# Two orders of instructions in a softmax-attention pipeline: the copy of the transposed probabilities ahead of the reciprocal on DVE, both heads' exponentials ahead of the copy of y on ACT

## The reference

```python
q = einsum('qdh,bcd->bhcq', Q, x) * sq;  k = ...;  v = ...      # x is the layer-normed input
att = einsum('bhcq,bhCq->bhcC', q, k) / d_query                  # 256 x 256 for each head, causal mask
p = softmax(att, axis=-1)
y = einsum('bhcC,bhCv->bhcv', p, v)
z = einsum('dvh,bhcv->bcd', W, y) * (sqrt(d_embed / d_value) / num_heads)
x = x + z;  x = x + 0.5 * spectral(layernorm(x))
```

## Time and profile before

| | |
|---|---|
| median of 3 runs | 1378.2 us (1377.81 to 1380.24) |
| the profiled execution | 1380.31 us, span 1378.6 us |
| mean granted TensorE clock | 0.994 of full speed |
| PE matmuls busy | 1298.8 us, 94% |
| DVE busy | 1017.6 us, 74% |
| ACT busy | 965.7 us, 70% |
| POOL busy | 586.5 us, 43% |

### The profile page before, as it was taken

The page is one execution under the profiler, slowest core; times in us unless marked ns, Lnnn a source line. Parts: engine busy times, 40 slices in busy tenths (PEclk is TensorE's granted clock), DMA queues, the critical chain, the costliest instruction groups (busy, mean ns, idle before and its releaser), DMA issues.

```text
span 1378.6 us, 38689 instructions
## 1 busy us (share of the span) xinstructions
PE 1298.8 (94%) x11323; PEld 1076.3 (78%) x11331; DVE 1017.6 (74%) x4813; ACT 965.7 (70%) x3377; POOL 586.5 (43%) x913
## 2 busy tenths in 40 slices
PE   5799977999999999999999999999999999999996
PEld 4688866878878787878787878787878787878885
DVE  7977789787777777777777777777777777777774
ACT  4744367587777777777777777777777777777774
POOL 5722157344444444444444444444444444444433
PEclk9999999999999999999999999999999999999999
DMA  8000000000000000000000000000000000000000
GB/s 204 0 1 0 1 0 2 0 2 2 2 10 0 9 0 9 0 9 0 9 0 9 0 9 0 9 0 9 0 9 0 9 0 9 0 9 0 9 1 17
DMA packets 14365, 12.33 MB, mean 9 GB/s; under 512 B 709, under 2 KB 12522, under 8 KB 14058
## 3 DMA queue, kind: packets, MB, share of 16 engines
q1 hardware_dynamic: 14240, 11.19, 3.0%
q10 hardware_dynamic: 10, 0.00, 0.0%
HBM read 7.00 MB, written 4.19 MB: 8 GB/s over the span
## 4 chain that ended last, share of the span: by engine, by line
PE 72%; DVE 13%; issue 9%; ACT 3%; DMA 1%; DVEq 1%; POOL 1%; SPq 1%; ACTq 0%; POOLq 0%
PE ps L1050 12%; PE ps L1020 10%; PE ps L1033 10%; PE ps L1059 9%; PE ps L1005 4%; PE ps L1039 4%; PE ps L1007 4%; PE ps L1006 3%; DVE ps L508 2%; DVE pT L523 2%; PE ps L1040 2%; PE ps L1041 2%; ACT qk_hi L730 2%; DVE neg_max L508 2%; PE ps L934 2%
## 5 line engine op out<-in xcount | busy, mean ns | idle before, releaser
L315 POOL TENSOR_TENSOR pr<-pr,rinv 128x256 f32<-128x256 f32 x256 | 157.4, 615 | 631.3 <-DVE rinv L516 631.3
L744 ACT ACTIVATE pr<-ps,neg_max 128x128 f32<-128x128 f32 (+1 forms) x1024 | 425.0, 425 | 0.0
L508 DVE CUSTOM_DVE_ANT_0 ps<-ps,mask 128x128 f32<-128x128 f32 (+1 forms) x1024 | 334.9, 386 | 0.0
L317 POOL TENSOR_TENSOR pr<-pr,rinv 128x512 f32<-128x512 f32 x256 | 266.9, 1043 | 0.0
L494 DVE TENSOR_TENSOR qk_lo<-ps,qk_hi 128x512 fp32r<-128x512 f32 x256 | 176.5, 689 | 104.2 <-ACT qk_hi L730 103.2
L1050 PE MATMUL ps<-pT,space 128*64 128x256 f32 (+1 forms) x2048 | 223.0, 339 | 24.0 <-DVE pT L523 20.9
L1033 PE MATMUL ps<-ident,pr 128*128 128x128 f32 x1536 | 218.9, 275 | 1.7 <-POOL pr L317 1.6
L744 ACT ACTIVATION_READ_ACCUMULATOR pr<-ps,neg_max 128x1 f32 x1024 | 211.7, 207 | 0.0
L730 ACT CAST qk_hi<-ps 128x512 fp32r<-128x512 f32 x256 | 150.4, 587 | 76.7 <-PE ps L1007 70.7
L1050 PEld LDWEIGHTS ps<-pT,space 128*64 128x64 f32 x2048 | 124.2, 136 | 100.1 <-DVE pT L523 36.3
L1033 PEld LDWEIGHTS ps<-ident,pr 128*128 128x128 f32 x1536 | 174.9, 140 | 34.8 <-issue 11.4
(11 more groups left out here) (165 smaller groups left out, 2398.0 us busy)
## 6 DMA issues: line engine op xcount, KB each, us to landing
out<-x_all SPq DMA_DIRECT2D x16, 256.0 KB, 2.3
x_all<-L_attn_x SPq DMA_DIRECT2D x1, 768.0 KB, 6.2
x_all<-L_attn_x SPq DMA_DIRECT2D x1, 512.0 KB, 3.9
space<-L_attn_Q SPq DMA_DIRECT2D x1, 512.0 KB, 15.3
space<-L_attn_K SPq DMA_DIRECT2D x1, 512.0 KB, 9.5
space<-L_attn_V SPq DMA_DIRECT2D x1, 512.0 KB, 11.3
space<-L_attn_W SPq DMA_DIRECT2D x1, 512.0 KB, 11.7
dft_s<-dft SPq DMA_DIRECT2D x1, 192.0 KB, 2.9
```

Of the source, the lines that this page charges most:

```text
L317: nc.gpsimd.tensor_tensor(pr[:, j, :, 1:3, :].rearrange("p h b k -> p h (b k)"), pr[:, j, :, 1:3, :].rearrange("p h b k -> p h (b k)"), r[ ...
L508: last = nc.vector.tensor_tensor_reduce(o, o, mask[:, T - w:T], -1.0, -MASKED, ALU.add, ALU.min, neg_max[:, j, 2 * h + qt:2 * h + qt + 1])
L744: last = nc.scalar.activation(dst, ps[:, BANK_S + 2 * j + h, qt * P:qt * P + w], ACT.Exp, bias=neg_max[:, j, at:at + 1], scale=-1.0, accum ...
```

## The change

On DVE the copy `probs_T(n-1)` now comes ahead of the reciprocal `inv_sum(n)` in each turn. On ACT both heads' exponentials of pair n+1 now come ahead of the copy of y. No instruction is added or removed, and no wait is changed; each moves with its instruction.

```diff
@@ vector engine, batch()
                     n, j = b * PAIRS + p, p % 2
-                    inv_sum(n, j)
                     if not (first and p == 0):
                         probs_T(n - 1, 1 - j)
+                    inv_sum(n, j)
                     if not (last and p >= PAIRS - 3):
                         qk_low(n + 3, 1 - j)
@@ scalar engine, batch()
                     if not (last and p >= PAIRS - 1):
                         exp_head(n + 1, 1 - j, 0)
+                        exp_head(n + 1, 1 - j, 1)
                     if p > 0:
                         y_out(b, jb, p - 1)
                     elif not first:
                         y_out(b - 1, 1 - jb, PAIRS - 1)
-                    if not (last and p >= PAIRS - 1):
-                        exp_head(n + 1, 1 - j, 1)
```

## The result

The changed kernel takes 1425.1 us (median of 4, 1421.58 to 1427.71), the kernel before 1378.6 in the same session: 1.0334 times as long, 95% interval 1.031 to 1.0359. The profiled execution took 1425.29 us with a span of 1423.5, so it is 45.0 us longer than that of before. The forecast was 1414, 36 us more than before, with a range from 1400 to 1428, which holds the result; the measured difference of the medians is 46.5 us.

What follows compares the result with a forecast made beforehand. PE, busy 94% of the span, was taken to bound the kernel. 13 jump batches x 0.80 + 19 ordinary x 1.33 = 35.7 us more gave 1414 us against the runs' median, range 1400 to 1428.

Steps and rivals of the forecast that it cites:

- PE's chain and the two waits of the transposes: PE bounds; its first transpose needs POOL's second multiplication, its fifth ACT's y copy, 2.57 us after `qk_high` starts.
- p = 0, 0.45: Turn p = 0: the fifth load, now 2.12 us after `qk_high`, waits for the later y copy, a stall of 0.45 us.
- p = 2, 0.60 with the y chain of 0.37 beside it: Turn p = 2: later reciprocal delays POOL and PE's first transpose by 0.60 us; y chain's 0.37 lies beside it, not added.
- p = 3, 0.46, and p = 4, -0.18: Fifth load in p = 3 comes 0.46 us later; in p = 4 the products' stall of 0.18 comes back.
- p = 4 to 7, nothing: Values turns: the chain of 2.57 us just fits into 2.63, 0.06 to spare, so nothing is counted.
- The room of 0.4: p = 4 to 7: POOL ends 3.0 us after the fifth load, the next turn's first load comes 3.4 after it.
- A batch with a jump, 0.80: Batch following the loop's jump back: 0.60 + 0.46 - 0.18 - 0.08 = 0.80 us, with p = 0's 0.45 vanishing in p = 1's wait.
- values turns that tip: Upper bound: half of a 0.18 us idle in each of 124 turns of p = 4 to 7, 11 us, making 1425.
- Rival 1: p = 4 to 7 stall too, about 0.1 x 124 = 12 us more, 1426; chance 0.13.
- Rival 2: Most of the delay is absorbed where PE already stands still; half of 35.7 hidden gives 1396; chance 0.12.
- Rival 3: Faster: probabilities copy comes 0.08 us earlier in p = 4 and after each jump, 3.6 us less, 1374.6; chance 0.06.
- The rule weighed against the trace: DVE's next instruction waits for an empty pipeline: p = 2's stall would be 0.69, total about 3 us more; not followed.

Runs made afterwards that it cites:

- the run with the small copy: The changed kernel with one small copy (128 x 1) put on ACT ahead of the y copy in p = 4 to 7: 1424.0 us.

## Why the prediction was right, and where it was not

- **PE's chain and the two waits of the transposes**: right. The chain from `qk_high` to the fifth load was worked out as 2.57 and is 2.58.
- **p = 0, 0.45**: measured 0.42, and 0.42 from the ACT part alone, in which POOL has no share.
- **p = 2, 0.60 with the y chain of 0.37 beside it**: measured 0.60, and 0.39 when the reciprocal is put back in that turn alone. That one is hidden in the other is shown. (In the trace of before the fifth load starts 0.39 after the first and not 0.44, so the y chain had 0.42 to cost.)
- **p = 3, 0.46, and p = 4, -0.18**: measured 0.47 and -0.17. An ordinary batch was summed at 1.33 and grew by 1.31.
- **p = 4 to 7, nothing**: right for the turns, with more cover than the 0.06 counted, as the run with the small copy shows. The room of 0.4 that I gave POOL there is wrong for p = 4, where DVE comes late from the statistics of p = 3. The room is then gone, as the run with the copy first in p = 1 and p = 4 shows. The changed kernel hides this, since PE reaches that turn 0.46 later.
- **A batch with a jump, 0.80**: this is the term that was mis-sized. It measured 1.18. The stalls of p = 2, 3 and 4 came as forecast; what failed is the step by which "the 0.45 of p = 0, and a POOL product that comes 0.60 later, vanish in that wait", and the copy "comes 0.08 earlier". They do vanish, since PE waits for the copy behind each jump still, but for 0.43 to 0.65 us and not "about 0.3": the copy comes later, as DVE's second gap falls ahead of `qk_low` where it had fallen behind it. Putting the reciprocal first in p = 0 alone brings 0.48 back. That is 13 x 0.38 = 4.9 of the 9.3 us by which the sum of 35.7 fell short of the profiled difference of 45.0.
- **The end**: not in the sum. There the turns have no query and key product, POOL and the copy follow each other in a closed chain, and PE waits for both: 2.2 us, and 3 more in executions in which the clock falls.
- The rest is small and of the other sign: five batches at the edges were counted with 1.33 each and cost 1.2.
- **The range**: that it held the result is luck in part. Its upper end came from 11 us for values turns that tip, which cost nothing; the jump and the end, which the sum had too low by 4.9 and 5.2, took that place.
- **Rival 1** (the values turns tip) didn't come true: 3.96 in each. Its time of 1426 was met for other reasons. **Rival 2** (absorbed) holds only for PE's own 0.23 at the jump. **Rival 3** (the earlier copy gains) fell by direct test: even in p = 1 and p = 4 alone the kernel is 0.27% slower.
- The rule weighed against the trace: the reciprocal starts 0.60 after a copy recorded with 0.68 (p = 2 above), so the two overlap in the changed kernel too, and the stall of 0.60 was sized rightly by the rows. The prediction took the rule as one without exception; the same section of the Trainium skill's page "VectorE: DVE Perf Modes" adds that an instruction which isn't held starts earlier, and the trace shows an earlier start.

## What to carry to other kernels

Where engines meet in a fixed round of turns, list for each wait of the bounding engine how much room it has in each kind of turn, and move only what is shorter than that room: an exponential that ACT could do while it waited anyway was free, the next one cost 30 us. An input that the bounding engine waits for isn't mended by giving it the place of a short instruction from which a longer chain starts; look at what else stands ahead of both. Here the statistics that stood there, moved by one turn, took all of PE's wait in p = 4 away, 5.5 us, and the kernel became some 8 us shorter. A sum over the steady loop must be followed by one over the loop's jump and one over the last turns, where the work that hid things is missing.

## What the runs showed of the hardware

- DVE's gaps behind a loop's jump have a place in the instruction stream: 1.7 to 2.1 us ahead of the first instruction, and a second one of 0.8 to 1.1 us behind `qk_low`, or of 1.4 to 1.6 us ahead of it when the two instructions at the start changed places. I didn't find what sets the place.
- A longer loop body made the jump dearer for engines that had shown no gap: PE 3.1 us and ACT 2.2 us at each of six jumps with four batches in a pass. For ACT eight more small copies in a body of two batches were enough: 2.1 us at each of 13 jumps.
- Behind the six jumps at which PE's weight loads stood still for some 3 us, the granted clock fell to 0.50 four times and stayed at 1.00 twice. A fall cost 1.3 us.
- The granted clock fell to 0.50 at the end of some executions and not of others with the same order of instructions there, after turns in which PE stood still twice, for 0.78 and for 0.91 us. In the kernel before, with single stalls of 0.94 us behind each jump, no slice of the page in the middle of the span shows it below nine tenths.
